# Causal attention scores issued in pairs: two heads behind one wait and one signal

## The chip, the cores and the metric

The kernel runs on one core of a Trainium2 chip. The metric is the device time of one execution in microseconds. Before the change the median of three runs is 1828.15 us (1825.17 to 1832.34).

## What is computed

The reference is a sandwich of four attention-like layers and four feed-forward layers, each wrapped as `x = x + layernorm(f(layernorm(x)))`, on x of 2 x 1024 tokens by 128 features. The change touches only the first attention layer, causal softmax attention with 16 heads of 8 features:

```python
Q = _rope(split_heads(x @ W_q.T)); K = _rope(split_heads(x @ W_k.T)); V = split_heads(x @ W_v.T)
score = jnp.einsum('bnqd,bnkd->bnqk', Q, K) / jnp.sqrt(jnp.float32(D_K))
score = jnp.where(causal[None, None], -jnp.inf, score)
attn = jax.nn.softmax(score, axis=-1)
out = jnp.einsum('bnqk,bnkd->bnqd', attn, V)
```

## The kernel before

The causal attention works on 8 groups (`NG`) of 4 heads (`HG`). PE (the matrix engine), ACT (exponentials) and DVE (maxima) each run their own function (`pe_attend0`, `act_attend0`, `dve_attend0`), and the order of the work is the program order of each, tied together by counting semaphores.

A group has two interleaved passes. The **maximum pass** (`pe_max` L596 to L620, `dve_max` L622 to L634) computes scores with queries on partitions, two heads at a time in two banks of 512 columns, and DVE reduces both to row maxima. It runs one group and ten units ahead, two units to a step, and ends in group 6. The **exponential pass** walks `STEPS` (L561): 12 steps to a group, each one block of 128 keys against a half of 512 queries. The steps are four blocks on the diagonal of the first half (512, 384, 256 and 128 columns), then, for the second half, block 0 (512), four diagonal blocks (512, 384, 256, 128) and three full ones (512). Within a step `pe_attend0` (L766) issues, in this order: a maximum unit, the scores of heads 0 and 1 (`pe_scores(..., 0)`), the first part of the weighted sum of the step before (`pe_weighted`, L706 to L726), another maximum unit, the scores of heads 2 and 3 (`pe_scores(..., 1)`), and the second part.

`pe_scores` (L676 to L693) makes for each head one matmul of 50 contraction rows (L687) and, on diagonal blocks, two mask matmuls of 64 columns (L691) accumulated onto it. The operands of head x lie on partitions 64x and up, so the two heads of a pair use different row halves of the PE array. The transposed scores of matmul number n go to bank `RING0[n % 3]`, a ring of three banks (4, 5 and 7). Matmul n waits until exponential n-3 has read its bank (L686), and each head signals `b_mm` when it is done (L693). Maximum units already issue both heads' matmuls and then both heads' masks, behind one wait and with one signal.

`act_weights` (L695 to L704) waits for the probability buffer of its step, then takes the four heads in turn: wait for `b_mm`, one exponential of 128 partitions by up to 512 columns from the bank into `PB` (L703), signal `b_exp`. After the step with which a half begins, ACT also copies the finished output bank (`act_out0`, L733), and the first weighted sum of the new half (L723) waits for that copy, since both use bank 6. A weighted sum waits for all four exponentials of its step (L714).

`sp_load0` (L825 to L828) holds the loads of queries and keys of group g until the scores of group g-3 are through, by the count of `b_mm`.

Of the kernel before, what the change touches and what calls it, by code (L numbers as in the profile page):

```python
# [18 lines left out]
P = 128  # L19
# [10 lines left out]
HG = 4  # L30
# [35 lines left out]
def sandwich(nc, x, w, cols, rows, rope, fc1q, fc2q, s2row, l1int, l2fc, r2w, r2b, moe2, moe2sel,  # L66
             r3w, r3b, moe3a, moe3b, consts, out):
    ctx = ExitStack()
    with ctx:
# [51 lines left out]
        def bank(i, a=0, b=CH):  # L121
            return PS[:, i * CH + a:i * CH + b]
# [23 lines left out]
        def rounded(at, n):  # L146
# [12 lines left out]
        K0 = [ARENA[:, 8192 + S * i:8192 + S * i + S].bitcast(BF16).rearrange("p (a n) -> p a n", a=2)  # L159
              for i in range(3, 6)]  # L160
# [225 lines left out]
        A = {}  # L386
# [131 lines left out]
        def sp_load_group(sp, L, q, k, g, par):  # L518
            for x in range(2):
                for dst, src in ((q, qx), (k, kx)):  # L520
                    sp.dma_start(dst[64 * x:64 * x + ROWS, :, :], group_rows(src, g, x))\
                      .then_inc(A[L, f"ld{par}"], 16)
# [39 lines left out]
        NSTEP = len(STEPS)  # L562
# [4 lines left out]
        RING0 = (4, 5, 7)  # L567

        MASKQ = [masks[:, P * i:P * i + P] for i in range(2)]
        MASKK = [masks[:, 2 * P + P * i:2 * P + P * i + P] for i in range(2)]  # L570
        EYE64 = masks[:, 4 * P:4 * P + P // 2]
# [5 lines left out]
        def step_cols(s):  # L577
            qh, kt = STEPS[s]
            return max(0, kt * P - qh * CH)
# [96 lines left out]
        def pe_scores(pe, g, s, p):  # L676

            qh, kt = STEPS[s]
            q0 = step_cols(s)
            diag = kt // TPC == qh  # L680
            for x in range(2):
                n = HG * (NSTEP * g + s) + 2 * p + x
                at = RING0[n % 3]
                r = slice(64 * x, 64 * x + ROWS + SHIFT0)
                if n >= 3:
                    pe.wait_ge(A[0, "b_exp"], n - 2)  # L686
                ins = pe.matmul(bank(at, q0), K0[g % 3][r, p, kt * P:kt * P + P],  # L687
                                Q0[g % 3][r, p, qh * CH + q0:qh * CH + CH], start=True, stop=not diag)
                r = slice(64 * x, 64 * x + 64)
                for half in range(2 if diag else 0):  # L690
                    ins = pe.matmul(bank(at, q0 + 64 * half, q0 + 64 * half + 64), MASKK[half][r, :], EYE64[r, :],  # L691
                                    start=False, stop=half == 1)
                ins.then_inc(A[0, "b_mm"], 1)  # L693

        def act_weights(act, g, s):  # L695
            q0 = step_cols(s)
            t = NSTEP * g + s
            if t >= 3:
                act.wait_ge(A[0, "pv"], t - 2)
            for h in range(HG):  # L700
                n = HG * t + h
                act.wait_ge(A[0, "b_mm"], n + 1)
                act.activation(PB[t % 3][:, h, q0:CH], bank(RING0[n % 3], q0), ACT.Exp, scale=SCORE_SCALE)\  # L703
                   .then_inc(A[0, "b_exp"], 1)  # L704

# [60 lines left out]
        def pe_attend0(pe):  # L766
            slots = Slots()

            def unit(m):
                pe_max(pe, slots, m)  # L770
                if turn_due(m) is not None:
                    pe_max_turn(pe, slots, turn_due(m))

            for m in range(NMAX + LEAD):
                unit(m)
            for g in range(NG):
                for s in range(NSTEP):
                    t = NSTEP * g + s
                    m = NMAX * (g + 1) + LEAD + 2 * s
                    unit(m)  # L780
                    if s == 0:
                        pe.wait_ge(A[0, f"m_ld{g % 3}"], 32 * (g // 3 + 1))
                    pe_scores(pe, g, s, 0)
                    if t:
                        pe_weighted(pe, t - 1, 0)
                    unit(m + 1)
                    pe_scores(pe, g, s, 1)
                    if t:
                        pe_weighted(pe, t - 1, 1)
                    if out_due(g, s) is not None:  # L790
                        pe_out0(pe, slots, out_due(g, s))
            pe_weighted(pe, NSTEP * NG - 1, 0)
            pe_weighted(pe, NSTEP * NG - 1, 1)
            pe_out0(pe, slots, QH * NG - 1)
# [20 lines left out]
        def act_attend0(act):  # L815
            for g in range(NG):
                for s in range(NSTEP):
                    act_weights(act, g, s)
                    if s == 0 and g:
                        act_out0(act, QH * g - 1)  # L820
                    if s == TPC:
                        act_out0(act, QH * g)
            act_out0(act, QH * NG - 1)

        def sp_load0(sp, g):  # L825
            if g >= 3:
                sp.wait_ge(A[0, "b_mm"], HG * NSTEP * (g - 2))
            sp_load_group(sp, 0, Q0[g % 3], K0[g % 3], g, g % 3)  # L828

        def sp_attend0(sp):  # L830
            sp_stack(sp, 0, 0)
            sp.wait_ge(A[0, "ones"], 1)
            for g in range(3):
                sp_load0(sp, g)
            sp_stack(sp, 0, 1)
            sp_max_rows(sp, 0)
            for g in range(NG):
                if g + 1 < NG:
                    sp_max_rows(sp, g + 1)
                if g + 3 < NG:  # L840
                    sp_load0(sp, g + 3)
# [1473 lines left out]
```

## Time and profile before

| what | value |
|---|---|
| median of three runs | 1828.15 us |
| profiled execution, its own time | 1824.99 us |
| its span, first to last instruction | 1823.2 us |
| mean granted PE clock | 0.853 of full |
| PE busy | 1407.1 us (77%) |
| ACT busy | 1156.1 us (63%) |
| DVE busy | 1092.7 us (60%) |
| L703, exponentials, x384 | 164.2 us busy, idle before them 102.9, of it 92.9 for L691 |
| L687, scores, x384 | 80.1 us busy, idle before them 5.0 |

The profile is of one execution. Engines are PE (matmul), PEld (its weight loads, which overlap), DVE, ACT, POOL and SP. A group of instructions is named by its line; idle time is the time its engine stood still before it, put down to what ended last. Busy PE time is not PE at its peak, since matmuls overlap. A timeline row that merges several instructions (x2, x4) gives the first start and the time to the last end.

### The profile page before, as it was taken

Reading aid. Unit: us, or ns where it says so; the run is one execution under the profiler, and the core shown is the slowest. Engines: PE = TensorE matmul, PEld = TensorE weight load, DVE = VectorE, ACT = ScalarE, POOL = GpSimd, SP = SyncE. Lnnn points to the kernel's source line nnn. Section 1 sums busy time; section 2 is a strip of 40 time slices with the busy share of each in tenths; the row PEclk is TensorE's granted clock in tenths of the full one; section 3 lists DMA queues with packets and bytes.
Section 4 is the critical chain, followed back from the end, with each engine's and each line's share of the span. In section 5 each row is a group of like instructions: output and inputs, shape, how many; then the busy total and the mean of one; then the engine's idle time right before and its main releaser. Section 6 shows DMA issues by size and latency. Waiting matters only on the chain.

```text
span 1823.2 us, 22552 instructions
## 1 busy us (share of the span) xinstructions
PE 1407.1 (77%) x8323; PEld 713.9 (39%) x8360; DVE 1092.7 (60%) x2034; ACT 1156.1 (63%) x1630; POOL 243.4 (13%) x343
## 2 busy tenths in 40 slices
PE   5388888587577777777777868939998986887886
PEld 3133333354011111111112446627666664565664
DVE  5778883431356656465574474358776684456787
ACT  3057777543799999999996343325455354657775
POOL 3200003320000000000000451130101215302000
PEclk9589999786587888878778677959999998889999
DMA  2700100001400000000002100000000002000000
GB/s 93 191 20 20 37 20 2 1 0 32 142 18 1 18 18 12 7 18 18 1 0 74 80 1 1 1 0 1 1 1 1 1 1 98 1 1 1 1 13 12
DMA packets 22176, 43.58 MB, mean 24 GB/s; under 512 B 3185, under 2 KB 7537, under 8 KB 21298
## 3 DMA queue, kind: packets, MB, share of 16 engines
q1 hardware_dynamic: 22066, 42.14, 8.2%
q8 instruction: 66, 1.08, 0.3%
q14 instruction: 44, 0.36, 0.1%
HBM read 28.37 MB, written 13.76 MB: 23 GB/s over the span
## 4 chain that ended last, share of the span: by engine, by line
PE 43%; ACT 22%; DVE 17%; issue 12%; POOL 3%; DMA 1%; SPq 1%; ACTq 0%; POOLq 0%; DVEq 0%
ACT SHARED L933 13%; PE PS L1512 5%; PE PS L1514 4%; PE PS L1513 4%; PE PS L544 4%; PE PS L890 4%; PE PS L723 4%; PE PS L877 3%; DVE NM L632 3%; DVE SHARED L943 2%; PE PS L546 2%; PE PS L612 2%; ACT ROUNDED L1888 2%; PE PS L687 2%; PE PS L1088 2%
## 5 line engine op out<-in xcount | busy, mean ns | idle before, releaser
L933 ACT ACTIVATE SHARED<-PS 128x1536 f32<-128x1536 f32 (+1 forms) x352 | 466.1, 1434 | 39.6 <-PE PS L877 38.6
L877 PE MATMUL PS<-QS,KS 51*128 51x512 bf16 (+1 forms) x1024 | 242.1, 461 | 148.2 <-ACT SHARED L933 128.4
L943 DVE TENSOR_TENSOR SHARED<-SHARED 128x1536 f32<-128x1536 f32 (+1 forms) x176 | 286.6, 1704 | 94.2 <-ACT SHARED L933 94.2
L1512 PE MATMUL PS<-ROUNDED 128*128 128x512 f32 x556 | 255.7, 460 | 49.0 <-DVE ROUNDED L1956 14.6
L703 ACT ACTIVATE SHARED<-PS 128x512 f32<-128x512 f32 (+3 forms) x384 | 164.2, 493 | 102.9 <-PE PS L691 92.9
L1514 PE MATMUL PS<-ROUNDED 128*128 128x512 f32 x556 | 225.2, 405 | 0.0
L1513 PE MATMUL PS<-ROUNDED 128*128 128x512 f32 x556 | 224.3, 403 | 0.0
L877 PEld LDWEIGHTS PS<-QS,KS 51*128 51x128 bf16 (+1 forms) x1024 | 41.2, 99 | 400.6 <-ACT SHARED L933 359.3
L890 PE MATMUL PS<-SHARED,Vg 128*16 128x512 f32 x1024 | 157.9, 694 | 1.7 <-DVE SHARED L943 1.6
L632 DVE TENSOR_REDUCE NM<-PS 128x2 f32<-128x1024 f32 (+3 forms) x128 | 128.9, 1021 | 38.9 <-PE PS L618 30.8
L1512 PEld LDWEIGHTS PS<-ROUNDED 128*128 128x128 f32 x556 | 110.3, 198 | 68.3 <-DVE ROUNDED L1956 21.4
L1602 ACT ACTIVATE KS<-PS 128x512 f32<-128x512 f32 x100 | 59.9, 599 | 114.8 <-PE PS L1514 114.8
L1514 PEld LDWEIGHTS PS<-ROUNDED 128*128 128x128 f32 x556 | 108.7, 196 | 25.7
L1513 PEld LDWEIGHTS PS<-ROUNDED 128*128 128x128 f32 x556 | 109.4, 197 | 20.7 <-issue 0.5
L1642 DVE TENSOR_TENSOR SHARED<-KS,PS 128x512 f32<-128x512 f32 x100 | 68.4, 684 | 78.9 <-ACT KS L1602 58.5
L317 POOL TENSOR_SCALAR VEY<-MVY 128x4 f32<-128x4 f32 x32 | 7.4, 232 | 741.9 <-DVE MVY L262 741.1
L612 PE MATMUL PS<-SHARED 48*128 48x512 bf16 (+3 forms) x384 | 70.3, 365 | 42.2 <-DMA SHARED<-kx 19.2
L723 PE MATMUL PS<-SHARED,Vg 128*16 128x256 f32 (+3 forms) x1152 | 91.8, 391 | 11.1 <-ACT SHARED L703 9.6
L440 POOL COPY Vg<-XH 128x256 f32<-128x256 f32 x16 | 6.4, 401 | 673.7 <-PE PS L890 429.5
L348 ACT ACTIVATE XN<-X,NBX,RSX 128x128 f32<-128x128 f32 x96 | 39.5, 482 | 84.4 <-POOL NBX L333 84.4
L374 PE MATMUL PS<-ident,XN 128*128 128x128 f32 x144 | 34.6, 387 | 67.0 <-ACT XN L348 67.0
L687 PE MATMUL PS<-SHARED 50*128 50x512 bf16 (+3 forms) x384 | 80.1, 334 | 5.0 <-ACT SHARED L703 4.6
(264 smaller groups left out, 2207.4 us busy)
## 6 DMA issues: line engine op xcount, KB each, us to landing
qx<-SHARED SPq DMA_DIRECT2D x24, 256.0 KB, 5.6
kx<-SHARED SPq DMA_DIRECT2D x24, 256.0 KB, 5.7
SHARED<-in_moe SPq DMA_DIRECT2D x3, 1600.0 KB, 12.4
SHARED<-qx SPq DMA_DIRECT2D x16, 192.0 KB, 4.5
SHARED<-kx SPq DMA_DIRECT2D x16, 192.0 KB, 5.2
QS<-qx SPq DMA_DIRECT2D x16, 192.0 KB, 4.5
KS<-kx SPq DMA_DIRECT2D x16, 192.0 KB, 4.9
SHARED<-in_moe3a SPq DMA_DIRECT2D x1, 1536.0 KB, 8.8
```

Of the source, the lines that this page charges most:

```text
L612: ins = pe.matmul(PS[:, slot(k, x):slot(k, x) + n], q[r, p, qt * P:qt * P + P], key[r, p, hi * CH:hi * CH + n], start=True, stop=not diag)
L632: dve.tensor_reduce(out=dst, in_=src, axis=AX.X, op=ALU.max, negate=True).then_inc(A[0, "a_red"], 1)
L687: ins = pe.matmul(bank(at, q0), K0[g % 3][r, p, kt * P:kt * P + P], Q0[g % 3][r, p, qh * CH + q0:qh * CH + CH], start=True, stop=not diag)
L703: act.activation(PB[t % 3][:, h, q0:CH], bank(RING0[n % 3], q0), ACT.Exp, scale=SCORE_SCALE)\
L723: ins = pe.matmul(PS[32 * h:32 * h + VC, 6 * CH + a:6 * CH + b], Vg[g % 2][:, kt, h, :], PB[t % 3][:, h, a:b], start=kt == 0, stop=last an ...
L877: ins = pe.matmul(bank((v % 2) * GRP + f - a), KS[g % 2][r, h // 2, kt * P:kt * P + P], QS[g % 2][r, h // 2, qh * CH:(qh + 1) * CH], start ...
L890: ins = pe.matmul(PS[32 * h:32 * h + VC, 6 * CH:7 * CH], Vg[g % 2][:, kt, h, :], EX[:, f * CH:f * CH + CH], start=kt == 0, stop=kt == KT - 1)
L933: act.activation(dst, PS[:, (v % 2) * GRP * CH:((v % 2) * GRP + b - a) * CH], ACT.Exp if second == qh else ACT.Sigmoid, scale=SCORE_SCALE)\
L943: dve.tensor_tensor(ex_tile(j), ex_tile(j), GR[w % RING][:, 0:(b - a) * CH], ALU.mult)\
L1512: pe.matmul(dst, w[0], x[0], start=start, stop=False)
L1513: pe.matmul(dst, w[0], x[1], start=False, stop=False)
L1514: return pe.matmul(dst, w[1], x[0], start=False, stop=stop)
```

## The change

`pe_scores` takes both heads of a pair together: one wait for `b_exp`, now for exponential n-2 where n is the pair's first number, so that both banks are free; then both score matmuls, then the masks of both heads alternating, and one signal on the last matmul. `b_mm` therefore counts pairs. ACT waits for it only at heads 0 and 2 of a step, and SP's count for the loads is halved. The banks, the ring, the number of matmuls and exponentials, and every other wait stay as they are.

```diff
@@ pe_scores
+            n = HG * (NSTEP * g + s) + 2 * p
+            at = [RING0[(n + x) % 3] for x in range(2)]
+            if n >= 2:
+                pe.wait_ge(A[0, "b_exp"], n - 1)
             for x in range(2):
-                n = HG * (NSTEP * g + s) + 2 * p + x
-                at = RING0[n % 3]
                 r = slice(64 * x, 64 * x + ROWS + SHIFT0)
-                if n >= 3:
-                    pe.wait_ge(A[0, "b_exp"], n - 2)
-                ins = pe.matmul(bank(at, q0), K0[g % 3][r, p, kt * P:kt * P + P],
+                ins = pe.matmul(bank(at[x], q0), K0[g % 3][r, p, kt * P:kt * P + P],
                                 Q0[g % 3][r, p, qh * CH + q0:qh * CH + CH], start=True, stop=not diag)
-                r = slice(64 * x, 64 * x + 64)
-                for half in range(2 if diag else 0):
-                    ins = pe.matmul(bank(at, q0 + 64 * half, q0 + 64 * half + 64), MASKK[half][r, :], EYE64[r, :],
-                                    start=False, stop=half == 1)
-                ins.then_inc(A[0, "b_mm"], 1)
+            for half in range(2 if diag else 0):
+                for x in range(2):
+                    r = slice(64 * x, 64 * x + 64)
+                    ins = pe.matmul(bank(at[x], q0 + 64 * half, q0 + 64 * half + 64), MASKK[half][r, :],
+                                    EYE64[r, :], start=False, stop=half == 1)
+            ins.then_inc(A[0, "b_mm"], 1)
@@ act_weights
-                act.wait_ge(A[0, "b_mm"], n + 1)
+                if h % 2 == 0:
+                    act.wait_ge(A[0, "b_mm"], n // 2 + 1)
@@ sp_load0
-                sp.wait_ge(A[0, "b_mm"], HG * NSTEP * (g - 2))
+                sp.wait_ge(A[0, "b_mm"], HG // 2 * NSTEP * (g - 2))
```

## Rows read from the trace of the kernel before

**Rows 1.** The first line of the profile's page.

```profile
span 1823.2 us, 22552 instructions
```

**Rows 2.** Stretches: from:to, length, busy us (xinstructions) by engine, PE clock, DMA share, GB/s.

```profile
97.00:332.00 235.00, 208.31 (x2855) 88.11 (x2851) 158.49 (x227) 170.04 (x400) 16.81 (x9) 0.98 0.10 19
...
185.70:215.20 29.50, 26.25 (x381) 11.34 (x378) 23.63 (x34) 21.26 (x51) 0.40 (x1) 1.00 0.15 30
```

**Rows 3.** Waits, 97 to 332 us: who <- for whom: us, times, longest.

```profile
ACT SHARED L703 <- PE PS L691: 92.9, 85, 41.3
...
PEld PS L687 <- ACT SHARED L703: 21.8, 57, 0.9
...
ACT SHARED L703 <- PE PS L687: 6.9, 15, 0.7
```

**Rows 4.** Timeline at step 7: start us, us, engine, line, op [idle before <-releaser].

```profile
206.06 0.29 PE L687 MATMUL PS<-SHARED 50*128 50x256 bf16 x2
206.18 0.23 PE L691 MATMUL PS<-masks 64*128 64x64 bf16 x4
```

**Rows 5.** Timeline at steps 4 and 5 of group 3.

```profile
196.60 0.60 ACT L703 ACTIVATE SHARED<-PS 128x512 f32<-128x512 f32 x1 [0.63 <-PE PS L687]
...
196.96 0.68 PE L687 MATMUL PS<-SHARED 50*128 50x512 bf16 x2
197.25 0.09 PEld L687 LDWEIGHTS PS<-SHARED 50*128 50x128 bf16 x1 [0.22 <-ACT SHARED L703]
...
197.57 1.09 ACT L703 ACTIVATE SHARED<-PS 128x512 f32<-128x512 f32 x2
...
198.52 0.63 ACT L733 ACTIVATE OS<-PS 128x512 f32<-128x512 f32 x1
...
199.25 0.62 PE L723 MATMUL PS<-SHARED,Vg 128*16 128x512 f32 x4 [0.58 <-ACT SHARED L703]
```

**Rows 6.** Timeline at steps 9 and 10 of group 3.

```profile
208.47 0.64 PE L687 MATMUL PS<-SHARED 50*128 50x512 bf16 x2
208.73 0.09 PEld L687 LDWEIGHTS PS<-SHARED 50*128 50x128 bf16 x1 [0.37 <-ACT SHARED L703]
...
208.95 0.60 ACT L703 ACTIVATE SHARED<-PS 128x512 f32<-128x512 f32 x1
...
209.70 0.38 PE L687 MATMUL PS<-SHARED 50*128 50x512 bf16 x2
...
210.12 1.09 ACT L703 ACTIVATE SHARED<-PS 128x512 f32<-128x512 f32 x2
...
211.25 0.41 PE L723 MATMUL PS<-SHARED,Vg 128*16 128x256 f32 x4
```

**Rows 7.** Timeline at step 0 of group 0.

```profile
98.17 0.94 PE L687 MATMUL PS<-SHARED 50*128 50x512 bf16 x2
98.51 0.10 PEld L687 LDWEIGHTS PS<-SHARED 50*128 50x128 bf16 x1 [0.21 <-ACT SHARED L703]
...
98.35 1.17 ACT L703 ACTIVATE SHARED<-PS 128x512 f32<-128x512 f32 x2
```

**Rows 8.** Timeline at steps 9 to 11 of group 7, the last.

```profile
322.48 0.09 PEld L687 LDWEIGHTS PS<-SHARED 50*128 50x128 bf16 x1 [0.46 <-ACT SHARED L703]
...
323.14 0.10 PEld L687 LDWEIGHTS PS<-SHARED 50*128 50x128 bf16 x2 [0.21 <-ACT SHARED L703]
...
324.06 1.08 ACT L703 ACTIVATE SHARED<-PS 128x512 f32<-128x512 f32 x2
...
324.22 0.09 PEld L687 LDWEIGHTS PS<-SHARED 50*128 50x128 bf16 x1 [0.50 <-ACT SHARED L703]
...
328.94 0.41 PE L723 MATMUL PS<-SHARED,Vg 128*16 128x256 f32 x4 [0.62 <-ACT SHARED L703]
```

**Rows 9.** Stretches at the end of group 6, columns as in rows 2.

```profile
298.00:300.00 2.00, 1.90 (x15) 0.41 (x19) 0.00 (x0) 1.40 (x4) 0.00 (x0) 0.65 0.01 4
300.00:302.00 2.00, 2.00 (x18) 0.26 (x12) 0.00 (x0) 1.51 (x3) 0.00 (x0) 0.50 0.00 0
```

## Prediction, made before the changed kernel was run

> **What bounds the kernel now.** The first reading is the profiled execution's own time against its span: 1824.99 us against 1823.2 [rows 1], so 1.8 us lie around the span, and the execution is 3.2 us below the median of the three runs shown, 1828.15. Sums below are made on the profiled execution and then put on the median. About 0.5% (9.1 us) is what a measurement of this kernel can tell from no change.
>
> The second reading is busy time by stretch. The causal pass lasts from 97 to 332 us, 235 us or 13% of the span. In it PE is busy 208 us, ACT 170, DVE 158; one steady head group of 29.5 us has PE 26.3, DVE 23.6, ACT 21.3 [rows 2]. So PE's stream is the nearest thing to a bound, and ACT has 8 us of slack in each group. There are 8 groups of 12 steps of 2 pairs: 192 pairs of scores, 384 exponentials.
>
> The third reading is who waited for whom there [rows 3]. ACT waited 100 times for scores. In the other direction, only 57 weight loads of scores waited for an exponential, 21.8 us in all. These 57 are the places where the three-bank ring bites, and where the change can act at all: at the other pairs both banks are free long before PE arrives.
>
> The fourth reading is the order of time around one pair, to see what happens to the two heads today.
>
> **The change part by part.**
>
> *Both heads' matmuls side by side, masks after them.* In the code of before, the masks of head 0 stand between the two score matmuls. In the trace both L687 matmuls start at 206.06 and the four mask matmuls follow at 206.18 [rows 4]: where nothing waits, the second head already runs beside the first. So the new order gives nothing here, and I take 0. The Trainium skill says otherwise in "TensorE: Matmul & The Clock Gate", Part 3, "The mechanism": matmuls go in strict program order, start and end. By that rule head 1 of before would start behind head 0's masks, and the change would win its overlap; the trace disagrees, since a matmul that stands later in the program starts first.
>
> *One signal for two.* The exponential of head 0 now waits for the last matmul of the pair instead of its own. Where the two run together they end within the resolution of the rows: no cost. From the matmul's end to ACT's start there are 0.04 us (209.70 + 0.38 to 210.12 [rows 6]), so what one signal less could give back lies between 0 and 0.04 us a pair; I take 0, as no row shows two signals queuing.
>
> *One wait for two banks.* Pair n, n+1 now waits for exponential n-2; before, matmul n waited for n-3 and only matmul n+1 for n-2. The second matmul is therefore released when it was before, and so is everything queued behind it on PE (weighted sums, the next maximum pass): nothing on PE moves by itself. What is late is matmul n, and with it exponential n. It costs time only where ACT was ready for it. From the start of matmuls to the start of their exponential there are 0.42 us (209.70 to 210.12), or 0.48 at the first pair of a step (208.47 to 208.95) [rows 6].
>
> The price at each kind of split pair, in program order:
>
> (a) Step 4, second pair. The first matmul started at 196.96; the load of the second waited until 197.25 (the exponential of 196.60 took 0.60). Exponential n started at 197.57 as the third of a row without gaps; now it starts at 197.25 + 0.42 = 197.67, 0.10 later. Behind it on ACT stands the copy out of the output bank at 198.52, and PE waits for that copy until 199.25, having idled 0.58 [rows 5]. So 0.10 us go through to PE. The pattern is there in groups 0 to 6: 7 x 0.10 = 0.7 us.
>
> (b) Step 9, first pair. The first matmul started at 208.47, the second load at 208.73. Exponential n moves from 208.95 to 208.73 + 0.48 = 209.21 and ends at 209.81; the next pair, issued at 209.70, now waits for it and starts at 209.86, which is 0.16 later. Its exponentials (two in 1.09 from 210.12) ended at 211.21 and the weighted matmuls started at 211.25 [rows 6]: they move by the same 0.16. Groups 0 to 5: 6 x 0.16 = 1.0 us.
>
> (c) Group 0, step 0, second pair, at half clock: matmuls at 98.17 and 98.51, first exponential at 98.35 + 1.17 - 0.60 = 98.92 [rows 7]. The first matmul reaches ACT 0.34 later, and the weighted sum behind waits: 0.3 us.
>
> (d) The tail, where the maximum pass has run out and PE catches up with ACT. A second load waits 0.46 us for its exponential at 322.48 [rows 8]; this happens three times (group 6 step 9, group 7 steps 4 and 9). There exponential n started at that same moment (the next pair's loads, released by it, came at 323.14; less 0.05 and 0.60 that is 322.49). Now it comes 0.48 after the load of 322.48, at 322.96, ends at 323.56 and releases the next pair at 323.61: 0.47 each. In steps 10 and 11 it repeats: the second load at 324.22 reaches ACT at 324.70, where the exponential started at 324.06 + 1.08 - 0.60 = 324.54, so 0.16 more, and the weighted sum of 328.94 that closes the pass, itself waiting for ACT, takes the total [rows 8]. So 3 x 0.47 + 0.16, and 0.1 for a pair split by 0.2 us at the start of group 7: 1.7 us.
>
> *Splits that cost nothing.* In each steady group five more pairs are split (steps 1, 2, 5, 6 and 10), and exponential n moves by up to 0.16 there. At steps 1 and 5 ACT is busy with the output copy anyway; at 2 and 6 the next scores are issued well after their bank is free; at 10 the 0.16 of (b) closes the gap. If that cover were gone, each would cost up to 0.16.
>
> *The SP wait* for Q and K loads is rescaled (24 for 48 a group) and falls on the same matmul: 0. On ACT the even heads keep their wait, the odd heads lose one already satisfied: 0.
>
> **Sum:** 0.7 + 1.0 + 0.3 + 1.7 = 3.7 us slower, 1828.7 for the profiled execution, 1831.9 on the median. That is 0.2%: no difference that could be measured.
>
> **Rivals.**
>
> *The ring locks (slower).* Mechanism: at 512 columns a pair that is held costs a whole round trip, 0.60 for the exponential, 0.05 to the load and 0.42 to 0.48 back, 1.07 to 1.13 us, against two exponentials every 0.97 (1.09 - 0.60 = 0.49 apart [rows 5]). That is 0.10 to 0.16 on each held pair. If all 57 waits of [rows 3] were on the path at 0.16, it would be 9.1 us: 1837.3, just at the bound; it becomes measurable only if delays also create new splits. A worse tail can help it: PE's clock fell to half in the sparse end of group 6: granted 0.65 from 298 to 300, 1.4 us of it at half, and 0.50 from 300 to 302 [rows 9]. Such a fall, 3.4 us long, costs at most half of that, 1.7 us, and longer PE gaps invite a second one. For it: the tail, where the delays do chain. Against it: in steady groups PE has its own work between, and two of seven splits pass through.
>
> *The signals were worth something (faster, small).* If an increment or a wait costs what lies between a matmul's end and ACT's start, at most 0.04 us at each of the 100 times that ACT waited [rows 3]: 4.0 us less, 1824.1. For it: PE-bound stage, 192 signals and 192 waits fewer. Against it: the rows show two matmuls of a pair starting together, with a wait on each. The Trainium skill has this rule too, in the same page, "The cost: per-tile semaphore tail": about 26 ns for each increment. By that, 100 of them would be 2.6 us, an estimate from the page; no row here shows the tail.
>
> *The masks did hold head 1 back (faster, large).* If the starts in the rows misled, 128 diagonal pairs would win up to 0.1 each (206.06 to 206.18, the step from scores to masks [rows 4]), 13 us: 1815. Against it stands the row itself.
>
> **How the numbers follow.** My case, a loss of 1 to 6 us: 0.65. The ring locks: 0.16, of which 0.06 beyond 0.5%. Signals worth something or nothing at all moved: 0.16, of which 0.01 beyond 0.5%. Masks: 0.03, nearly all beyond. So faster 0.04, same 0.90, slower 0.06. Low end: the signals' rival, 1824.1. High end: all waits on the path and one or two more clock falls, 1837.3 + 2.7 = 1840. The three runs alone spread by 7 us, which fits inside.
>
> **What would show it.** If right: the pass is 2 to 6 us longer than its 235; no second load of a pair waits alone, both start within 0.01 us; the gap of 0.58 before the weighted sum of step 5 grows to about 0.68; the waits of L687 loads for ACT grow in time though not in number; everything from 332 us on keeps its length. Wrong on the small side: gaps between exponentials unchanged and PE's stream shorter. Wrong on the large side: exponentials in steady groups that start every 1.1 us in pairs with a gap each time, DVE then waiting more for L618, or a granted clock that falls again before 332.

## The result, and the profile after

| | before | after |
|---|---|---|
| median of six runs each | 1830.46 us | 1839.77 us |
| lowest to highest | 1825.17 to 1833.26 | 1837.78 to 1841.23 |
| profiled execution, own time | 1824.99 us | 1840.93 us |

The ratio of after to before is 1.0061, 95% interval 1.0044 to 1.0078: slower by 0.6%, some 8 to 14 us (the medians differ by 9.3). The measured median lies at the very top of the range given (1824 to 1840); the forecast itself, 3.7 us and no measurable difference, was wrong.

The page of the changed kernel: its first line, the PE clock over the span in 40 slices (tenths; 9 is 90% or more), and the exponentials' group, where [rows 1] and the table of before have their counterparts. The last line is the PE clock of the kernel before.

```profile
span 1839.1 us, 22552 instructions
...
PEclk9579999785588787887878678859999998889999
...
L705 ACT ACTIVATE SHARED<-PS 128x512 f32<-128x512 f32 (+3 forms) x384 | 167.7, 490 | 115.5 <-PE PS L692 102.8
...
PEclk9589999786587888878778677959999998889999
```

The span grew by 15.9 us over [rows 1], more than the medians did, since the profiled execution of before, 1824.99 us, lies below all six runs of its kernel, and that of the changed kernel among the slowest of its own. All of the growth lies in the causal pass: the last exponential starts at 344.07 us against 328.30, 15.8 later, and from there to the end both take 1495 us. PEclk hardly shows it: the six slices that hold the pass read 8 9 9 9 9 7 before and 7 9 9 9 9 7 now. The granted clock of each group shows more.

The pass cut at the first exponential of each head group (columns as in [rows 2]): groups 0, 1, 3, 5, 6 and 7.

```profile
97.15:130.66 33.51, 30.03 (x361) 11.54 (x361) 23.39 (x32) 21.32 (x49) 0.00 (x0) 0.76 0.02 4
130.66:161.63 30.97, 27.07 (x381) 10.85 (x377) 23.91 (x34) 21.69 (x50) 0.40 (x1) 0.94 0.14 28
...
192.84:224.05 31.21, 27.08 (x381) 10.86 (x377) 23.81 (x34) 21.70 (x50) 0.40 (x1) 0.95 0.15 28
...
255.09:284.98 29.89, 25.69 (x381) 10.64 (x377) 23.82 (x34) 21.70 (x51) 0.40 (x1) 1.00 0.14 28
284.98:315.80 30.82, 25.88 (x331) 9.39 (x327) 14.63 (x23) 21.69 (x50) 14.81 (x4) 0.89 0.01 3
315.80:345.00 29.20, 22.36 (x266) 7.73 (x262) 1.10 (x4) 21.70 (x50) 0.00 (x0) 0.88 0.00 1
```

A steady group took 29.5 us before at PEclk 1.00 [rows 2]. Here group 5 takes 29.89, also at 1.00: that is 0.35 us more, the lateness of which 0.26 had been worked out. Groups 1 and 3 take 30.97 and 31.21 at 0.94 and 0.95. Each of them holds one stretch of 3.4 us at 1.2 GHz, half of 2.4, and group 0 holds one of 10.2 us. So two things are in the result, and the second is the larger.

Who waited for whom, 97 to 348 us, beside [rows 3]:

```profile
ACT SHARED L705 <- PE PS L692: 102.8, 93, 41.2
...
PEld PS L687 <- ACT SHARED L705: 38.4, 72, 1.1
...
PE PS L687 <- ACT SHARED L705: 14.0, 36, 0.7
```

Score loads now wait 72 times for an exponential, not 57, and 38.4 us, not 21.8 (the prediction had the time growing and the number not); ACT waits 102.8 us for the pair's last mask, not 92.9.

Steps 4 and 5 of group 5, where the clock is full, beside [rows 5]:

```profile
265.21 0.60 ACT L705 ACTIVATE SHARED<-PS 128x512 f32<-128x512 f32 x1 [0.64 <-PE PS L687]
...
265.86 0.10 PEld L687 LDWEIGHTS PS<-SHARED 50*128 50x128 bf16 x2 [0.26 <-ACT SHARED L705]
...
266.29 0.60 ACT L705 ACTIVATE SHARED<-PS 128x512 f32<-128x512 f32 x1
...
266.95 0.39 PE L687 MATMUL PS<-SHARED 50*128 50x512 bf16 x2 [0.34 <-ACT SHARED L705]
...
267.27 0.60 ACT L735 ACTIVATE OS<-PS 128x512 f32<-128x512 f32 x1
...
267.97 0.62 PE L725 MATMUL PS<-SHARED,Vg 128*16 128x512 f32 x4 [0.57 <-ACT SHARED L705]
```

The step reads as it was worked out. Both loads start at 265.86 in one row of x2. The exponential follows 0.43 later, 1.08 after the one of 265.21, where it came 0.97 after its counterpart before (196.60 to 197.57). Counted from that first exponential, the copy at 267.27 and the weighted sum at 267.97 are later by 0.14 and 0.11. One sign that the prediction named did not come: PE's idle time before the weighted sum stays at 0.57 (0.58 before) and does not grow to 0.68. What is new is 0.34 us of idle time ahead of step 5's first scores, at 266.95, where the joint wait now holds both heads.

The same place in group 3:

```profile
205.02 0.60 ACT L735 ACTIVATE OS<-PS 128x512 f32<-128x512 f32 x1
...
205.72 1.05 PE L725 MATMUL PS<-SHARED,Vg 128*16 128x512 f32 x4 [0.57 <-ACT SHARED L705]
```

Four weighted matmuls that took 0.62 us in [rows 5] take 1.05: the clock has just fallen. Here is the stretch ahead of that fall and the one in it, first of the changed kernel, then the matching stretch of the kernel before (lined up by the first exponential of group 3).

```profile
201.90:205.30 3.40, 2.42 (x28) 0.86 (x28) 3.24 (x5) 2.76 (x7) 0.00 (x0) 1.00 0.02 5
205.30:208.70 3.40, 2.98 (x22) 0.78 (x22) 0.83 (x2) 1.30 (x3) 0.00 (x0) 0.50 0.00 0
```

```profile
195.50:198.90 3.40, 2.78 (x28) 1.16 (x28) 3.24 (x5) 2.75 (x7) 0.00 (x0) 1.00 0.02 5
```

PE was busy 2.42 of 3.40 us where it had been busy 2.78, with the same 28 matmuls; then the clock is at half.

### The profile page after: what moved, and what is told of

It is laid out like the page before. It is cut to its first block, busy times and chain, and to the rows that moved or that the text cites. A ratio compares the mean times of both kernels' runs of the same rounds, so it can differ in the third digit from the quotient of the medians.

```text
span 1839.1 us, 22552 instructions
## 1 busy us (share of the span) xinstructions
PE 1414.5 (77%) x8323; PEld 709.2 (39%) x8360; DVE 1094.0 (59%) x2034; ACT 1160.1 (63%) x1630; POOL 243.6 (13%) x343
## 3 DMA queue, kind: packets, MB, share of 16 engines
q8 instruction: 66, 1.08, 0.2%
## 4 chain that ended last, share of the span: by engine, by line
PE 43%; ACT 24%; DVE 16%; issue 12%; POOL 3%; DMA 1%; SPq 1%; ACTq 0%; POOLq 0%; DVEq 0%
ACT SHARED L935 13%; PE PS L1514 5%; PE PS L1516 4%; PE PS L1515 4%; PE PS L544 4%; PE PS L892 4%; PE PS L725 3%; ACT SHARED L705 3%; PE PS L879 3%; DVE SHARED L945 2%; PE PS L546 2%; DVE NM L632 2%; PE PS L1090 2%; ACT ROUNDED L1890 2%; PE PS L687 2%
## 5 line engine op out<-in xcount | busy, mean ns | idle before, releaser
L705 ACT ACTIVATE SHARED<-PS 128x512 f32<-128x512 f32 (+3 forms) x384 | 167.7, 490 | 115.5 <-PE PS L692 102.8
L725 PE MATMUL PS<-SHARED,Vg 128*16 128x256 f32 (+3 forms) x1152 | 98.9, 418 | 11.5 <-ACT SHARED L705 9.0
L1884 ACT ACTIVATE SHARED<-PS,C 128x512 f32<-128x512 f32 x64 | 44.1, 689 | 59.3 <-PE PS L1516 59.2
```

Source lines behind the costliest of these rows:

```text
L725: ins = pe.matmul(PS[32 * h:32 * h + VC, 6 * CH + a:6 * CH + b], Vg[g % 2][:, kt, h, :], PB[t % 3][:, h, a:b], start=kt == 0, stop=last an ...
```

## The experiments

The first four tell apart which part of the edit costs, and whether the clock is a cause or only goes along. The kernel before was run again beside them: its median was 1826.02 us beside e1 to e4, 1827.02 beside e5 to e8 and 1826.90 beside e9 and e10, where it was 1830.46 beside the changed kernel. So the ratios, which are those on record, say more than a difference of medians of two batches. Where falls of the clock are counted, it is in the one profiled execution of each kernel.

### e1: the wait alone

```diff
-                if n >= 3:
-                    pe.wait_ge(A[0, "b_exp"], n - 2)
+                if x == 0 and n >= 2:
+                    pe.wait_ge(A[0, "b_exp"], n - 1)
```

> The kernel before with one edit: the first matmul of a pair waits for exponential n-2, as the second does; order, masks and the two signals stay. Theory A (the joint wait starts both matmuls together and late; exponential n comes later, PE's work is bunched, and PE's clock falls to half once a group near step 5): about the changed kernel, 1838 to 1841 us, steady groups of 31.2 us with one clock fall each. Theory B (the single signal is what costs): as before, 1828 to 1832, groups of 29.5. Theory C (the new order of the masks costs): as before too.

Measured: 1839.58 us (4 runs), ratio 1.0064 (1.0039 to 1.0089). Groups 0, 3 and 4:

```profile
97.31:130.75 33.44, 30.05 (x361) 11.65 (x361) 23.38 (x32) 21.30 (x49) 0.00 (x0) 0.76 0.02 4
...
190.37:220.18 29.81, 25.70 (x381) 10.72 (x377) 23.82 (x34) 21.68 (x50) 0.40 (x1) 1.00 0.14 29
220.18:251.31 31.13, 27.15 (x381) 10.93 (x377) 23.83 (x34) 21.68 (x50) 0.40 (x1) 0.95 0.15 29
```

The wait alone makes the whole loss, as far as the ratios tell. Its steady group at full clock is 29.81 us, 0.27 above 29.54 of before; (a) and (b) of the prediction add to 0.26. A group with a fall has 31.13. But of groups 0 to 5 only 0 (10.2 us) and 4 have falls in this execution of 1834.14 us, group 6 has one and group 7 two. The other three runs took 1839 to 1842, at a mean granted clock of 0.844 where this one had 0.848.

### e2: the single signal alone

```diff
-            if n >= 2:
-                pe.wait_ge(A[0, "b_exp"], n - 1)
             for x in range(2):
+                if n + x >= 3:
+                    pe.wait_ge(A[0, "b_exp"], n + x - 2)
```

> The changed kernel with the waits apart again (matmul n waits for exponential n-3, matmul n+1 for n-2), but with its order and its one signal for the pair. Exponential n is as late as in the changed kernel, while the first matmul runs early and alone as before. Theory A1 (the lateness of exponentials is what drops the clock): as the changed kernel, 1838 to 1841. Theory A2 (the bunching of PE's work drops it): only the lateness stays, 0.3 us a group and the tail, 1832 to 1835, groups of 29.9 with the clock full. Theory B: as the changed kernel.

Measured: 1838.32 us (4 runs), ratio 1.0062 (1.0042 to 1.0081). Groups 1 and 2:

```profile
129.14:158.99 29.85, 26.36 (x381) 10.92 (x385) 23.81 (x34) 21.68 (x50) 0.40 (x1) 1.00 0.15 30
158.99:190.17 31.18, 27.96 (x381) 11.16 (x385) 23.91 (x34) 21.68 (x50) 0.40 (x1) 0.95 0.14 28
```

Also the whole loss, though no matmul starts later by its own wait: exponential n is late because its signal comes with the last matmul of the pair. So wait and signal are not two costs that add. Each alone makes the first exponential of a split pair as late as the second matmul, and that lateness is the cost. Theory A2, bunching of PE's work, falls: here the first matmul still runs early, PE is busy 26.36 us in the group at full clock against 25.70 in e1, and the clock falls in three of the five groups 1 to 5. B, taken as the signal being the only culprit, falls with e1.

### e3: the new order alone

```diff
+            last = []
...
-                r = slice(64 * x, 64 * x + 64)
-                for half in range(2 if diag else 0):
-                    ins = pe.matmul(bank(at, q0 + 64 * half, q0 + 64 * half + 64), MASKK[half][r, :], EYE64[r, :],
-                                    start=False, stop=half == 1)
-                ins.then_inc(A[0, "b_mm"], 1)
+                last.append(ins)
+            for half in range(2 if diag else 0):
+                for x in range(2):
+                    at = RING0[(HG * (NSTEP * g + s) + 2 * p + x) % 3]
+                    r = slice(64 * x, 64 * x + 64)
+                    last[x] = pe.matmul(bank(at, q0 + 64 * half, q0 + 64 * half + 64), MASKK[half][r, :],
+                                        EYE64[r, :], start=False, stop=half == 1)
+            for ins in last:
+                ins.then_inc(A[0, "b_mm"], 1)
```

> The kernel before with the new order alone: both score matmuls, then both heads' masks alternating; a wait and a signal for each head as before. Theories A and B: as before, 1828 to 1832, groups of 29.5 us. Theory C: as the changed kernel. Where the first matmul runs early, its masks now come after the second matmul, so its exponential can be late by the same 0.1 to 0.26 us at diagonal steps; that alone would make 1 to 2 us at most.

Measured: 1826.25 us (10 runs), ratio 0.9999 (0.9984 to 1.0014). Groups 0, 3, 6 and 7:

```profile
97.52:127.19 29.67, 26.64 (x361) 10.88 (x361) 22.97 (x32) 21.11 (x49) 0.00 (x0) 0.91 0.02 4
...
186.25:215.78 29.53, 26.16 (x381) 10.89 (x385) 23.67 (x34) 21.52 (x51) 0.40 (x1) 1.00 0.15 30
...
274.83:302.51 27.68, 24.56 (x331) 9.67 (x335) 14.71 (x23) 21.27 (x51) 14.81 (x4) 1.00 0.01 3
302.51:328.10 25.59, 21.54 (x265) 7.96 (x268) 1.09 (x4) 21.25 (x50) 0.00 (x0) 1.00 0.00 1
```

The order costs nothing and gains nothing: 29.53 us a group. C falls, and so does the rival that masks had held head 1 back. Once risen in group 0, the clock of the profiled execution did not fall at all in the pass, group 6 included (27.68 us at 1.00), which gives the pass without the clock: group 6 of before, 28.60 with its one fall, had paid 0.9 for it.

### e4: the changed kernel, PE kept busy at step 5

```diff
-            for x in range(2):
+            again = s == TPC + 1 and p == 0
+            for i, x in enumerate((0, 1, 0, 1) if again else (0, 1)):
                 r = slice(64 * x, 64 * x + ROWS + SHIFT0)
                 ins = pe.matmul(bank(at[x], q0), K0[g % 3][r, p, kt * P:kt * P + P],
-                                Q0[g % 3][r, p, qh * CH + q0:qh * CH + CH], start=True, stop=not diag)
+                                Q0[g % 3][r, p, qh * CH + q0:qh * CH + CH], start=True,
+                                stop=not diag or again and i < 2)
```

> The changed kernel with the two score matmuls of step 5, first pair, issued twice (the same result written twice), in the place where PE otherwise stands idle 0.6 to 0.7 us for the output copy. Theory A: PE is busier in the stretch ahead of the fall, the clock falls of groups 1 to 4 go away, groups are 29.9 us instead of 31.2, and the kernel comes 4 to 6 us below the changed one, 1833 to 1836. If the clock only goes with the slowness and doesn't cause it, the added work gains nothing: 1840 to 1842.

Measured: 1830.77 us (10 runs), ratio 1.0026 (1.0012 to 1.0040). Groups 0, 3 and 6, then the stretch that matches the one ahead of the fall in the changed kernel:

```profile
98.26:128.47 30.21, 26.49 (x363) 10.76 (x363) 23.19 (x32) 21.31 (x49) 0.00 (x0) 0.89 0.02 5
...
188.23:218.12 29.89, 25.92 (x383) 10.74 (x379) 23.82 (x34) 21.70 (x51) 0.40 (x1) 1.00 0.15 29
...
277.88:307.38 29.50, 24.71 (x333) 9.27 (x329) 14.62 (x23) 21.70 (x51) 14.81 (x4) 0.94 0.01 3
```

```profile
197.30:200.70 3.40, 2.58 (x30) 0.96 (x30) 3.24 (x5) 2.77 (x7) 0.00 (x0) 1.00 0.00 0
```

Two useless matmuls for each group take 7 to 9 us off: e1 and e2, which cost as much as the whole edit, had medians of 1839.58 and 1838.32 in the same batch, and the ratio goes from 1.0061 to 1.0026. The falls of groups 0 to 4 are gone (one is left in group 6 and one in group 7), PE is busy 2.58 us there and not 2.42, and every steady group takes 29.88 us, what the one group without a fall (29.89) took in the changed kernel. The waits are as they were, so the clock is a cause, and what is left in these groups is the lateness. Not everything fits a simple reading of busy time, though; the stretch ahead of a fall in e2:

```profile
199.30:202.70 3.40, 2.77 (x28) 0.97 (x28) 3.25 (x5) 2.77 (x7) 0.00 (x0) 0.99 0.02 5
```

PE was busy 2.77 us, as much as before, and the clock fell at 202.7. So PE's busy time in a profile doesn't say when the clock will fall; what the chip looks at is left open.

### e5 and e6: lateness at some steps only

First e5, then e6, each from the kernel before:

```diff
-                    pe.wait_ge(A[0, "b_exp"], n - 2)
+                    pe.wait_ge(A[0, "b_exp"], n - 1 if x == 0 and s in (TPC, TPC + 1) else n - 2)
```

```diff
-                    pe.wait_ge(A[0, "b_exp"], n - 2)
+                    pe.wait_ge(A[0, "b_exp"], n - 1 if x == 0 and s >= 9 else n - 2)
```

> The kernel before with the first head's wait moved to exponential n-2 at steps 4 and 5 alone. The price worked out for step 4 is 0.10 us in groups 0 to 6 and 0.47 in group 7: 1.2 us if the clock stays. Theory A, refined (PE's idle time around the output copy of steps 4 and 5 is what makes the clock fall): falls appear in some of groups 0 to 4 and the kernel is 3 to 6 us above before. If the lateness of all steps together is needed: no fall ahead of group 6, and 1 to 2 us above before.

> The kernel before with the first head's wait moved to exponential n-2 at steps 9 to 11 alone. Worked out: 0.16 us in groups 0 to 5, 0.47 in group 6 and 0.63 in group 7, 2.1 us in all with the clock full, groups of 29.7 us. More falls than one in the tail, each worth about 1.3 us, would bring it to 3 or 4 us; falls in groups 1 to 4 are not expected by the refined theory A, as PE waits for DVE and not for ACT there.

Measured: e5 1830.57 us (10 runs), ratio 1.0026 (1.0011 to 1.0041); e6 1831.49 us (10 runs), ratio 1.0010 (0.9999 to 1.0021). Groups 3, 4 and 7 of e5, then 1, 3 and 7 of e6:

```profile
187.16:216.81 29.65, 25.96 (x381) 11.11 (x385) 23.68 (x34) 21.39 (x51) 0.40 (x1) 1.00 0.15 29
216.81:247.60 30.79, 27.31 (x381) 11.29 (x385) 23.67 (x34) 21.39 (x51) 0.40 (x1) 0.94 0.15 29
...
306.14:335.70 29.56, 24.90 (x265) 8.80 (x266) 1.10 (x4) 21.15 (x51) 0.00 (x0) 0.83 0.01 1
```

```profile
128.52:159.57 31.05, 27.82 (x381) 11.63 (x385) 23.82 (x34) 21.37 (x50) 0.40 (x1) 0.95 0.14 28
...
189.29:219.02 29.73, 26.39 (x381) 11.38 (x385) 23.82 (x34) 21.37 (x50) 0.40 (x1) 1.00 0.14 29
...
308.98:334.90 25.92, 20.88 (x262) 7.96 (x258) 1.10 (x4) 21.24 (x50) 0.00 (x0) 1.00 0.01 1
```

At full clock the prices come out: 29.65 less 29.54 is 0.11 for steps 4 and 5 (worked out: 0.10 for step 4 and nothing for step 5), 29.73 less 29.54 is 0.19 for steps 9 to 11 (worked out: 0.16). Group 7 of e6, without a fall, takes 25.11 us from its first to its last exponential (308.98 to 334.09), where before took 24.65 (303.65 to 328.30): 0.46 more, where 0.63 was worked out for steps 9 to 11. The refined theory, that it is the idle time of steps 4 and 5 that drops the clock, is not borne out as it was put: e5 has falls in groups 0 and 4 (and in 6 and 7, the last of 10.2 us), but e6 has them in groups 0 and 1, where it wasn't expected to, and two in group 6. Yet the place is the same in both. In the changed kernel, e1, e2, e5 and e6 every fall of groups 0 to 5 begins 11.9 to 13.2 us after the group's first exponential, around the output copy and step 5. That holds for e6 too, whose step 5 has its waits as before. How lateness at steps 9 to 11 leads to a fall there isn't shown.

### e7 and e8: the output copy on DVE

To take away PE's wait for the copy at step 5, `act_out0` becomes a DVE copy, after DVE's first maximum of step 4 and its second of step 0; e7 does it to the kernel before, e8 to the changed one.

```diff
-            act.activation(OS[:, :], bank(6), ACT.Copy).then_inc(A[0, "o_sb"], 1)
+            dve.tensor_copy(OS[:, :], bank(6)).then_inc(A[0, "o_sb"], 1)
...
                     unit(m)
+                    if s == TPC:
+                        dve_copy0(dve, QH * g)
                     unit(m + 1)
+                    if s == 0 and g:
+                        dve_copy0(dve, QH * g - 1)
```

> The kernel before with the copy out of the output bank on DVE (after its first maximum of step 4 and its second of step 0) instead of ACT, so that PE does not wait for it behind four exponentials. PE's wait ahead of the weighted sum of step 5 goes (0.58 us), the one at step 1 shrinks little, since DVE is late there: 0.5 us a group, 4 us in all, 1822 to 1825. If DVE's maxima get late by the copy instead and PE waits for them: no gain, or up to 0.6 us a group of loss.

> The changed kernel with the copy out of the output bank on DVE. Theory A: most of the loss hung on PE standing idle for that copy, so the clock falls of groups 1 to 4 go, groups are 29.5 us or less, and the kernel comes to 1827 to 1832, at most 4 us above the same edit on the kernel before. If the clock falls have nothing to do with that wait: they stay, and the kernel keeps 9 us or more above the same edit on the kernel before.

Measured: e7 1825.54 us (10 runs), ratio 0.9990 (0.9976 to 1.0004); e8 1835.30 us (10 runs), ratio 1.0037 (1.0022 to 1.0051). A steady group and 1380 to 1460 us, in the expert stage, of e7; the latter of the kernel before; groups 2 and 7 of e8:

```profile
155.18:184.18 29.00, 26.30 (x381) 11.36 (x385) 24.88 (x36) 20.40 (x49) 0.40 (x1) 1.00 0.15 30
1380.00:1460.00 80.00, 72.98 (x283) 50.33 (x282) 46.45 (x105) 34.66 (x60) 9.98 (x18) 0.89 0.00 1
```

```profile
1380.00:1460.00 80.00, 72.23 (x302) 50.43 (x306) 51.18 (x113) 37.34 (x64) 12.66 (x23) 0.98 0.00 1
```

```profile
156.84:186.17 29.33, 25.70 (x381) 10.61 (x377) 25.01 (x36) 20.92 (x49) 0.40 (x1) 1.00 0.15 30
...
303.48:330.30 26.82, 21.07 (x262) 7.08 (x258) 2.48 (x6) 20.91 (x48) 0.00 (x0) 0.94 0.01 1
```

In the pass both profiled executions do what was expected: 29.00 us a group, and 29.33 with the change, at full clock, again 0.33 for the lateness; in e8 the falls of groups 0 to 5 are gone, one is left in group 6 and one in group 7. But the profiled execution of e7 did not gain the 4 us. Its pass ends 5.1 us earlier (last exponential at 323.18) and the whole span is 2.6 longer. Far away, where nothing was edited, PE's clock is at 0.89 and not 0.98: it stood at half there for 17.0 us, in three stretches, where before had one of 3.4. The time is lost there: e7 comes to this stage 4.2 us ahead of before (the same ACT instruction at 1365.54 and 1369.77) and is 1.2 us behind some 95 us later. That e7 arrives earlier is not the reason. e8 comes to this stage in step with the kernel before (that ACT instruction at 1369.78) and has three stretches at half clock too. Here is its stage, then the DVE instruction at which the two part there, in e8 and in before:

```profile
1380.00:1460.00 80.00, 72.99 (x282) 50.32 (x281) 47.88 (x108) 34.00 (x58) 12.57 (x23) 0.89 0.00 1
...
1371.11 0.69 DVE L1644 TENSOR_TENSOR SHARED<-KS,PS 128x512 f32<-128x512 f32 x1 [1.22 <-ACT KS L1604]
...
1370.75 0.69 DVE L1642 TENSOR_TENSOR SHARED<-KS,PS 128x512 f32<-128x512 f32 x1 [0.86 <-ACT KS L1602]
```

The same instruction starts 0.36 us later in e8, with the ACT result it waits for at the same time, and it waits 1.21 us in e7 and 1.22 in e10. So the stretches go with the copy on DVE itself; why this instruction is late isn't shown. And e8's time missed the expectation: 1835.3, 10 us above e7, where its profiled execution (1831.81) is only 4 above. By the median it is the other outcome of the expectation, 9 us or more above e7, that came true. The mean granted clock is on record for each run: 0.844 to 0.847 in e8's five slowest, 0.849 in the profiled one. Whether the slower runs have their falls in the pass or later isn't seen, since one execution is profiled.

### e9: step 5 and the tail kept busy

```diff
+        def pe_fill(pe, slots, g, s, p):
+            if g < NG - 2 or NMAX * (g + 1) + LEAD + 2 * s < NMAX * NG + 2:
+                return
...
+            pe.wait_ge(A[0, "a_red"], slots.last_max)
+            for x in range(2):
+                r = slice(64 * x, 64 * x + ROWS + SHIFT0)
+                pe.matmul(bank(1 + 2 * x, q0), K0[g % 3][r, p, kt * P:kt * P + P],
+                          Q0[g % 3][r, p, qh * CH + q0:qh * CH + CH], start=True, stop=True)
```

> The kernel with the matmuls of step 5 issued twice, and in addition, where the maximum pass has run out (from step 8 of group 6 on), each pair of scores followed by the same two matmuls into banks that nobody reads. If the changed kernel's tail is slow mostly by its clock (group 7 took 28.3 us against 24.7 before): the falls after group 6 go, group 7 takes 25.5 to 26.2 us (lateness alone, 1.1 us by the prediction's working, and a little for the added work), and the kernel is 1 to 3 us below the fill of step 5 alone. If the tail is slow by its waits: group 7 stays at 27 us or above and the kernel at 1830 to 1832.

Measured: 1829.61 us (10 runs), ratio 1.0008 (0.9997 to 1.0019). Groups 3, 6 and 7:

```profile
187.98:217.87 29.89, 25.91 (x383) 10.74 (x379) 23.81 (x34) 21.69 (x50) 0.40 (x1) 1.00 0.15 29
...
277.64:306.24 28.60, 24.61 (x347) 9.26 (x339) 14.63 (x23) 21.70 (x51) 14.81 (x4) 1.00 0.01 3
306.24:333.30 27.06, 23.18 (x311) 7.76 (x310) 1.10 (x4) 21.69 (x50) 0.00 (x0) 1.00 0.01 2
```

With e4's edit and this one, the changed kernel has no fall in the pass after the rise in group 0, and it can't be told from the kernel before. The fair partner is e3, which has neither the lateness nor a fall: from first to last exponential e9 takes 234.6 us (98.01 to 332.64) and e3 229.7 (97.52 to 327.22), 4.9 us apart, against 3.7 worked out. Group 7 went from 28.27 to 26.40 us (306.24 to 332.64); expected were 25.5 to 26.2. The added matmuls have a price of their own: put into e7 (that is e10) they take group 7 from 23.83 to 25.16 us, both without a fall. If they cost the same 1.3 us here, an estimate, some 3.6 of the 4.9 are lateness.

### e10: the copy on DVE, and the tail kept busy

e7 with the added matmuls of e9 in the tail.

> The kernel before with the output copy on DVE and the same added matmuls in the tail. In the causal pass it should be 5 to 6 us shorter than before (29.0 us a group, no fall in the tail); whether the kernel as a whole gains depends on the clock of the expert stage after 1390 us, where the earlier run of the copy on DVE had three more stretches at half clock. Without them 1820 to 1823, with them 1825 to 1828.

Measured: 1825.11 us (12 runs), ratio 0.9986 (0.9975 to 0.9998). A steady group, and the expert stage:

```profile
155.90:184.88 28.98, 26.29 (x381) 11.36 (x385) 24.87 (x36) 20.41 (x48) 0.40 (x1) 1.00 0.16 31
1380.00:1460.00 80.00, 72.52 (x278) 50.35 (x280) 46.81 (x106) 33.68 (x57) 10.02 (x18) 0.89 0.00 1
```

Below before by 0.14%, hardly clear of noise, and not to be told from e7 (0.9990). The pass has no fall but is only 3.8 us shorter (97.92 to 324.52), where 5 to 6 were expected and e7 has 4.6 with one fall: the added matmuls cost more in group 7 (1.3 us) than they save in group 6 (28.20 in e7, 27.53 here). Part of the gain is given back in the expert stage at 0.89, as in e7.

## Why the prediction was wrong

**What bounds, and where the change acts.** Right for the split pairs: their prices in steady groups came out within 0.03 us. But score loads that wait grew in number too, from 57 to 72, and step 5's first scores now leave PE idle for 0.34 us, which the working had not seen.

**Both heads side by side: 0.** Right, by e3 (0.9999). The Trainium skill's rule of strict program order ("TensorE: Matmul & The Clock Gate", "The mechanism") would have had the new order gain; e3, where only the order changes, gains nothing.

**One signal, taken as 0.** A little off, and not as a gain. With the joint wait an exponential starts 0.43 us after its matmuls, not 0.42, and the changed group is 29.89 us against e1's 29.81: 0.08 us a group lost by the single signal, together with the new order, which alone is free. Without the joint wait the single signal costs as much as the whole edit (e2), so the account that split pairs pay through the wait was half of it: they pay by either. The rival of the signals, and the 26 ns for each increment that the Trainium skill gives ("TensorE: Matmul & The Clock Gate", "The cost: per-tile semaphore tail"), show no gain in any run here.

**One wait, (a) to (d): 3.7 us.** Right in mechanism, and near in size, at the clock it assumed.

| step | worked out | measured at full clock |
|---|---|---|
| (a) step 4 | 0.10 us a group | 0.11 (e5, steps 4 and 5) |
| (b) step 9 | 0.16 us a group | 0.19 (e6, steps 9 to 11) |
| (a) and (b) | 0.26 | 0.27 (e1), 0.35 with the signal (after) |
| tail, steps 9 to 11 of group 7 | 0.63 | 0.46 (e6) |
| whole pass | 3.7 | 4.9, with the added matmuls (e9 less e3) |

**The step that failed is the sum's silent assumption: that the durations of the trace of before, all of the pass but 3.4 us at the full clock, would stay.** The prediction did name the clock, but as a helper of the slower rival, "in the sparse end of group 6", "one or two more clock falls", and put against it that "in steady groups PE has its own work between". In the changed kernel the clock fell in groups 0, 1, 2, 3, 4, 6 and 7: after the rise in group 0 it stood at half for 37.4 us (10.2 + 4 x 3.4 + 3.4 + 3.4 + 6.8), before for 3.4. A fall of 3.4 us costs a steady group 1.1 to 1.3 us (30.97 and 31.21 less 29.88 in e4), below the bound of 1.7 that was given; it was the count that was off: eight falls, one of them of 10.2 us and one of 6.8, where the sum had the one of before and the high end one or two more. From first to last exponential the profiled execution of the changed kernel takes 246.9 us (97.15 to 344.07). Against e3's 229.7 that is 17.2: 4.9 as in e9, for lateness and e9's added matmuls together, and the other 12.3 for the clock, or more by what those matmuls cost. The kernel before, with its single fall, took 230.4 (97.86 to 328.30).

That the clock makes most of the loss, and isn't made by it, is shown by e4 and e9: they add work, leave every wait of the change in place, and bring the ratio of 1.0061 down to 1.0026 and 1.0008.

**Chances.** 0.06 for slower beyond 0.5% was too low. The ring did not lock: a steady group at full clock lost 0.35 us. What came true of that rival was its helper, the clock falls; that waits alone could hardly reach 0.5% (57 x 0.16 = 9.1 us) was rightly seen, and the weight should have gone by the clock. That the median still lies within the range is luck: its high end of 1840 is made of all 57 waits on the path and two falls at most, and neither is what happened.

**Left open.** What drops the clock. It goes with lateness at steps 4 and 5 or at 9 to 11, in groups 0 to 5 always around step 5, and PE's busy time in the stretch ahead doesn't tell (2.42 us and 2.77 ahead of falls, 2.58 and 2.78 without one). Whether the wait ahead of step 5's weighted sum is the deciding gap isn't settled either: e8 took it away and its profile has no fall in groups 1 to 5, but its median stayed high.

## What to carry to other kernels

Before joining two waits into one, look for the pairs in which the first member runs ahead today: the price is the lateness of what follows it, and in the steady groups here it came out to a few hundredths of a microsecond from the rows. One signal for two took the first member's lead away just as the joint wait did. And where PE runs at full clock with gaps, don't price a small added delay at that clock alone: 0.35 us a group of lateness went with 1.1 to 1.3 more in groups 1 to 4, and two repeated matmuls a group brought that back.

## What the runs showed that was not expected

- Two score matmuls that write a result twice, once a group, take back more than half of the loss (e4 1.0026, the changed kernel 1.0061).
- Either half of the edit costs as much as both (ratios 1.0064, 1.0062, 1.0061).
- A gain of 5.1 us in the causal pass (e7) went with more time at half clock some thousand microseconds later, in unedited code: 0.89 granted between 1380 and 1460 us and not 0.98. All three kernels with the copy on DVE have it (e7, e8, e10), e8 though it reaches that stage no earlier than the kernel before.
- A matmul of the second row half starts within 0.01 us of the first although two others stand between them in program order ([rows 4]), and e3 fits that: putting them side by side changes nothing.
